# Sharing key rows between tiles, halving the experts' lists, a silu from tanh, and normalized rows remade on chip

## What is computed

```python
xn = layernorm(x)
# attention: q, k, v = heads(xn @ W + b)
scores = (q @ k.T + rel_q + rel_k) / 4     # rel_q[l, r] = q[l] . emb[l - r + 255], rel_k[l, r] = k[r] . emb[...]
s = layer_norm(softmax(scores) @ v @ Wo + bo + xn) * gamma + beta
# experts: n = layer_norm(xn); x1 = xn + n + n @ mix_w + mix_b
y = sum over the two chosen e of w[e] * (silu(z @ w1[e] + b1[e]) @ w2[e] + b2[e])   # z = layer_norm(x1)
g = silu(x1 + y)
out = x + s * g
```

## Time and profile before

| | us |
|---|---|
| median of 3 runs (lowest, highest) | 1816.91 (1814.05, 1818.83) |
| the profiled execution | 1817.45 |
| its span, first to last instruction | 1815.8 |
| TensorE, VectorE, ScalarE, GpSimd busy in it | 1545.8, 1246.4, 1058.4, 583.0 |
| granted TensorE clock, mean share of full speed | 0.934 |

### The profile page before, as it was taken

How to read it: one execution, slowest core, us unless ns; L and a number is a source line. 1 busy time by engine, 2 the same in 40 slices (tenths; PEclk the granted TensorE clock), 3 DMA queues, 4 the chain that set the end, 5 groups by cost and what they waited for, 6 DMA issues and landing times.

```text
span 1815.8 us, 34886 instructions
## 1 busy us (share of the span) xinstructions
PE 1545.8 (85%) x12086; PEld 1164.0 (64%) x12086; DVE 1246.4 (69%) x3120; ACT 1058.4 (58%) x2250; POOL 583.0 (32%) x754
## 2 busy tenths in 40 slices
PE   5759630377999999998999999988999999999996
PEld 2324430366898889897988888955555555555553
DVE  6846643361466666666675667688998899998995
ACT  2425332122655555554555455289898888988983
POOL 1343456241110111110111011124353655636556
PEclk9879755688999999999999999999999999999998
DMA  6454338796899999899999987899989889898891
GB/s 218 162 177 157 134 100 255 192 200 220 251 325 346 313 336 382 283 329 393 391 375 331 374 293 268 301 340 346 302 282 339 304 294 345 281 345 302 294 318 47
DMA packets 218318, 510.49 MB, mean 281 GB/s; under 512 B 28480, under 2 KB 76096, under 8 KB 213664
## 3 DMA queue, kind: packets, MB, share of 16 engines
q1 hardware_dynamic: 193568, 411.58, 66.9%
q0 software_dynamic: 23424, 92.49, 14.6%
q10 hardware_dynamic: 1152, 4.19, 0.6%
HBM read 435.11 MB, written 195.82 MB: 347 GB/s over the span
## 4 chain that ended last, share of the span: by engine, by line
PE 55%; DVE 7%; issue 7%; DMA 5%; ACT 4%; POOL 3%; POOLq 0%; SPq 0%; DVEq 0%; ACTq 0%; another core or an unknown queue 0%
PE up L1120 12%; PE dn L1132 12%; PE rl L1100 11%; PE pt L1517 8%; PE sc L1509 4%; PE cx L1530 4%; DVE rel_out L1048 3%; DMA scratch_rel<-rel_out 2%; DMA rows<-scratch_sorted 2%; DVE probsT L1402 2%; PE wo_ps L1552 1%; ACT square L1359 1%; PE wo_ps L1555 1%; ACT square L1025 1%; PE tp L1108 1%
## 5 line engine op out<-in xcount | busy, mean ns | idle before, releaser
L1048 DVE TENSOR_TENSOR rel_out<-rl,square 128x1024 f32<-128x1024 f32 x256 | 402.5, 1575 | 231.1 <-PE rl L1100 208.8
L1025 ACT COPY square<-rl 128x1024 f32<-128x1024 f32 x256 | 259.5, 1016 | 273.8 <-DVE rel_out L1048 183.8
L1359 ACT ACTIVATE square<-square,row_least 128x512 f32<-128x512 f32 x512 | 365.8, 717 | 21.6 <-DVE row_least L1394 20.0
L1394 DVE CUSTOM_DVE_ANT_1 square<-sc,square 128x512 f32<-128x512 f32 x512 | 338.0, 686 | 36.0 <-issue 32.6
L1517 PE MATMUL pt<-ident,square 128*128 128x128 f32 x2048 | 316.1, 277 | 31.2 <-ACT probsT L1366 24.1
L1120 PE MATMUL up<-rowsT,w_b 128*128 128x128 f32 x2272 | 312.5, 284 | 8.7 <-DVE rowsT L1054 6.8
L1517 PEld LDWEIGHTS pt<-ident,square 128*128 128x128 f32 x2048 | 243.8, 142 | 111.6 <-DVE probsT L1402 36.8
L1132 PE MATMUL dn<-w_b,hid 128*128 128x256 f32 x1136 | 300.6, 393 | 0.0
L1120 PEld LDWEIGHTS up<-rowsT,w_b 128*128 128x128 f32 x2272 | 279.4, 195 | 11.0 <-DVE rowsT L1054 8.3
L1034 ACT ACTIVATE hid<-up,w_b 128x128 f32<-128x128 f32 x568 | 162.6, 372 | 147.9 <-PE up L1120 147.9
L1132 PEld LDWEIGHTS dn<-w_b,hid 128*128 128x128 f32 x1136 | 200.6, 194 | 18.2
(11 more groups left out here) (197 smaller groups left out, 1688.7 us busy)
## 6 DMA issues: line engine op xcount, KB each, us to landing
scratch_rel<-rel_out SPq DMA_DIRECT2D x256, 512.0 KB, 5.2
square<-scratch_rel SPq DMA_DIRECT2D x256, 512.0 KB
w_b<-in_w POOLq DMA_DIRECT2D x71, 1152.0 KB
w_b<-in_w POOLq DMA_DIRECT2D x71, 1028.0 KB
krows_sb<-scratch_stack SPq DMA_DIRECT2D x128, 192.0 KB, 4.9
krows_sb<-scratch_stack SPq DMA_DIRECT2D x128, 128.0 KB, 4.9
late_by_head<-scratch_parts SPq DMA_DIRECT2D x128, 128.0 KB
scratch_parts<-part SPq DMA_DIRECT2D x96, 128.0 KB
```

The source lines that it names most:

```text
L1025: nc.scalar.copy(dst, src).then_inc(s_kc, 1)
L1048: nc.vector.tensor_tensor(out[n % SRING][:], rl[r][:].rearrange("p a (b s) -> p (a b) s", s=TILE), square(tile)[:, u * UN:(u + 1) * UN], A ...
L1359: nc.scalar.activation(sm[j][:, i], sm[j][:, i], ACT.Exp, bias=least[:, j, i:i + 1], scale=-1.0, accum_out=es[:, g // 2 % 2, i, 2 * j + g ...
L1394: nc.vector.tensor_tensor_reduce(sm[j][:, i].rearrange("p (c s) -> p c s", c=LT), sc[i % 2][:].rearrange("p (c s) -> p c s", c=LT), rq[j][ ...
```

## The change

- `project` no longer stores the normalized rows. VectorE keeps each row's mean and inverse deviation (`means`, `invs`). `attention` loads only x, and GpSimd recomputes `xo` from it (`center`), so it waits for that load.
- The gate's silu is written as (1 + tanh(v / 2)) v / 2. ScalarE writes the tanh into `yg`; GpSimd adds 1 and multiplies with `ax` (`twice_silu`, at the end of each batch's round). The factor 1/2 goes once into gamma and beta.
- Block `jb` no longer stands at position jb of the experts' list: even blocks walk through positions 0 to 35, odd ones through 36 to 70 (`part_of`), each with its own weight slot. `fresh` compares neighbouring positions.
- The tiles go forward and backward by turns (`ORDER`), so that the last tile of a row and the first of the next share their key rows; these are loaded once (`RUN`), 13 x 8 pieces instead of 16 x 8. The ring has nine slots, four of them in `late_by_head`. The products begin at block 8.
- SyncE issues the first five key pieces between the loads of the late half, the stack store right after the repacks, and four key pieces and the query rows behind that. The clearing of `late_by_head` moves from block 10 to behind the store of block 68.

```diff
-FIRST_REL = 10
+EVEN = (NBLK + 1) // 2
+FIRST_REL = 8
-KRING = 5
+KRING = 9
+LATE_SLOTS = 4
+ORDER = [(lt, rt if lt % 2 == 0 else LT - 1 - rt) for lt in range(LT) for rt in range(LT)]
...
@@ project
-            def store_xn(b):
-                sp.wait_ge(s_xn, b + 1)
-                sp.dma_start(t["xn"][b * S:(b + 1) * S].rearrange("(p t) e -> p t e", t=ST), xn[:, b * ST:(b + 1) * ST]).then_inc(s_xs[b], 16)
...
+                if half == 1:
+                    step.did(nc.vector.tensor_copy(means[:, p * PAIR:(p + 1) * PAIR], mv[:, :, 0]))
+                    step.did(nc.vector.tensor_copy(invs[:, p * PAIR:(p + 1) * PAIR], y[:, 0:PAIR]))
@@ route
-                then(nc.vector.tensor_tensor(fresh_f[:, 2:NBLK], owner_f[:, 2:NBLK], owner_f[:, 0:NBLK - 2], ALU.not_equal))
+                then(nc.vector.tensor_tensor(fresh_f[:, 1:NBLK], owner_f[:, 1:NBLK], owner_f[:, 0:NBLK - 1], ALU.not_equal))
@@ experts
-        kst = [sb(f"krows_sb{i}", [KS, PIECE, BH], BF16) for i in range(KRING)]
+        kst = [sb(f"krows_sb{i}", [KS, PIECE, BH], BF16) for i in range(KRING - LATE_SLOTS)]
+        for late in by_head:
+            room = late[:].rearrange("k h l -> k (h l)").rearrange("k (n x h) -> k n x h", n=LATE_SLOTS // 2, h=BH)
+            kst += [room[:, i] for i in range(LATE_SLOTS // 2)]
...
+        RUN = [sum(ORDER[i][1] != ORDER[i - 1][1] for i in range(1, tile + 1)) for tile in range(TILES)]
+        LAST_OF = {run: tile for tile, run in enumerate(RUN)}
+        RT_OF = {run: ORDER[tile][1] for tile, run in enumerate(RUN)}
+        LOADS = len(LAST_OF) * PIECES
+        NEW_ROW = [tile == 0 or ORDER[tile][0] != ORDER[tile - 1][0] for tile in range(TILES)]
+        def used(x):
+            return LAST_OF[x // PIECES] * UNITS + (x % PIECES + 1) * PER_PIECE
...
-                    x = ((tile + 1) * UNITS + u) // PER_PIECE - 1 + KRING
-                    if u % PER_PIECE == 0 and x < TILES * PIECES:
+                    while x < LOADS and used(x - KRING) <= (tile + 1) * UNITS + u:
                         load_k(x)
...
+            def part_of(jb):
+                return jb // 2 + jb % 2 * EVEN
...
-                if jb == FIRST_REL:
-                    pool.wait_ge(s_br, B)
-                    for late in keep["late_by_head"]:
-                        nc.gpsimd.memset(late[:].rearrange("k h l -> k (h l)").bitcast(F32), 0.0).then_inc(s_gaps, 1)
...
+                if jb == LAST_REL:
+                    pool.wait_ge(s_kp, TILES * UNITS)
+                    for late in keep["late_by_head"]:
+                        nc.gpsimd.memset(late[:].rearrange("k h l -> k (h l)").bitcast(F32), 0.0).then_inc(s_gaps, 1)
@@ attention
+            step.did(nc.gpsimd.tensor_scalar(gb[:], gb[:], 0.5, None, ALU.mult))
+            def twice_silu(b):
+                own = ax[b % 2][:].rearrange("p t e -> p (t e)")
+                pool.wait_ge(s_g, b + 1)
+                tanh = yg[:].rearrange("p i k e -> p (i k e)")
+                step.did(nc.gpsimd.tensor_scalar(tanh, tanh, 1.0, None, ALU.add))
+                step.settle()
+                step.did(nc.gpsimd.tensor_tensor(own, own, tanh, ALU.mult))
+                step.settle()
...
             def reload(b):
                 after(pool, s_hh, 2 * b)
-                pool.dma_start(xo[:], t["xn"][b * S:(b + 1) * S].rearrange("(p t) e -> p t e", t=ST)).then_inc(s_xo, 16)
                 pool.dma_start(xx[:], t["x"][b * S:(b + 1) * S].rearrange("(p t) e -> p t e", t=ST)).then_inc(s_xx, 16)
+            def center(b):
+                pool.wait_ge(s_xx, (b + 1) * 16)
+                for i in range(ST):
+                    n = b * ST + i
+                    nc.gpsimd.tensor_scalar(xo[:, i], xx[:, i], means[:, n:n + 1], invs[:, n:n + 1],
+                                            ALU.subtract, ALU.mult).then_inc(s_xo, 1)
...
                 if b:
                     reload(b - 1)
+                    center(b - 1)
...
                 if b:
                     finish(b - 1)
+                twice_silu(b)
...
-                nc.scalar.activation(ax[b % 2][:], ax[b % 2][:], ACT.Silu).then_inc(s_g, 1)
+                nc.scalar.activation(yg[:].rearrange("p i k e -> p (i k e)"), ax[b % 2][:].rearrange("p t e -> p (t e)"), ACT.Tanh,
+                                     scale=0.5).then_inc(s_g, 1)
```

More of the change, by code:

```diff
@@ L154, in project @@
         s_ps = [sem(f"parts_stored{i}") for i in range(PRING)]
-        s_xs = [sem(f"xn_stored{i}") for i in range(B)]
         block = ctx.enter_context(nc.Block())
@@ L939, in sync @@
                 sp.dma_start(by_head[b % 2][:], src).then_inc(s_bh[b % 2], 16)
[L940 to L944 removed]
+                if b == 2:
+                    sp.wait_ge(keep["stack_stored"], 16 * 2)
+                if 2 <= b < 2 + KRING - LATE_SLOTS:
+                    load_k(b - 2)
             sp.wait_ge(s_br, B)
@@ L948, in sync @@
                 sp.dma_start(dst, by_row[:, i * TILE:(i + 1) * TILE]).then_inc(s_bs, 16)
+            x = KRING - LATE_SLOTS
+            while x < KRING:
+                load_k(x)
+                x += 1
+            for p in range(PIECES):
+                load_q(0, p)
             sp.wait_ge(s_bs, 16 * 2)
-            for p in range(PIECES - 1):
-                load_k(p + KRING)
+            while used(x - KRING) < UNITS:
+                load_k(x)
+                x += 1
             for tile in range(TILES):
```

56 lines of the change are left out of this document (25 added, 31 removed).

## The result

The changed kernel takes 1824.33 us (median of 6 runs, 1820.74 to 1829.81) where the kernel before takes 1815.73 (6 runs, 1811.84 to 1818.83): a ratio of 1.0049, 95% interval 1.0031 to 1.0066. It is slower by 8.6 us, where 1808 was forecast. The profiled execution took 1829.81 us, span 1828.1, against 1817.45 and 1815.8: +12.3 us to account for. (The profiled execution is the slowest of the six; by the medians it is 8.6.)

The account below looks back on a forecast made before the run. TensorE was taken to hold both long stages, so an edit is worth what it takes from TensorE's waits. Terms 0 - 2 - 17 + 3 - 18 + 10 + 15 = -9 gave 1808 us, range 1789 to 1828.

Parts of the forecast that it names:

- Stored rows gone: Before the experts: eight stores leave SyncE's queue, eight small copies enter VectorE's; 0 us, between -1 and +1.5.
- Blocks 0 to 7: First expert blocks: the earlier stack store may shorten TensorE's 11.27 us wait for rows; -2 us, between -6 and +4.
- Interleaved stretch: Experts with relative products: fewer doubled spots, two disturbed stretches go as weights load less often; -17 us, between -25 and -7.
- Clearing: Start of attention: SyncE's first loads wait until GpSimd has cleared the late rows; +3 us, between +1 and +5.
- GpSimd's additions: GpSimd's round in attention: doubled silu adds 5.6 us (3.9 to 6.1), centring 4.87 us plus the `xx` landing.
- Rival C: GpSimd is quicker: doubled silu 3.9 us, no wait in attention, tail +11; 1794 us, chance 0.20.
- wait at VectorE's addition: Attention, batches 2 to 6: centred rows come 42.9 us after the seed, wanted at 40.86; 2.1 us each, +10 us.
- The gate's -18: Attention's gates: tanh without table loads takes 2.57 of TensorE's 3.1 us wait, seven times; -18 us, between -21 and -15.
- The tail: From the last seed to the final addition: GpSimd's longer chain takes 102.2 us instead of 87.3; +15 us (+11 to +19).
- A: Rival: GpSimd's chain sets attention's period, centred rows 5.3 us late; +11 us, 1828 us, chance 0.15.
- B: Rival: the disturbed expert stretches come from query rows alone and stay, -7 instead of -17; 1818 us, chance 0.17.
- D: Rival: the change does not do what it says, tanh brings its own table loads; given no chance.

Follow-up runs that it names:

- last group: Three kernels timed together, before at 1783.49 us: a base with half lists, one with silu back (1764.04 us), one with normalized rows stored and reloaded (1754.74 us).
- third group: Four kernels timed together, before at 1782.71 us: a base and three undoing half lists (1772.88 us), tile order and shared key rows (1756.33), or both (1770.52).
- best_again: Changed kernel with x loaded ahead of the doubled silu and gathers, the last batch's ahead of the root and centred before that silu: 1760.50 us, 0.9881 of before.
- old_tiles: best_again with tiles row by row, key rows loaded for every tile and late rows cleared early; half lists stay: 1756.33 us, 0.9848 of before.
- base_silu: half_lists_base with silu and its table loads back on ScalarE, no doubled silu on GpSimd, centring kept: 1764.04 us, 0.9889 of before.
- half_lists_base: The old_tiles kernel timed again as a base: 1755.70 us, 0.9842 of before.
- experts_only: Changed kernel's expert stage with attention as before: normalized rows stored and reloaded, silu on ScalarE: 1811.32 us, 0.9946 of before.
- rows_reloaded: Changed kernel with normalized rows stored and loaded again, tangent gate and doubled silu on GpSimd kept: 1797.38 us, 0.9872 of before.
- first group: Four kernels timed together, before at 1820.94 us: changed kernel with gate, stored rows or both put back, or x loaded ahead; 1797.38 to 1811.32 us.
- silu_kept: Changed kernel with silu and its table loads back on ScalarE, rows still centred on chip: 1811.24 us, 0.9946 of before.
- rows_ahead: Changed kernel with x loaded once more, straight into `xo` ahead of the root on GpSimd, and centred in place behind it: 1802.10 us, 0.9895 of before.

## Why the prediction was wrong

**The path, step by step.** *Stored rows gone, 0*: right (1.0 us in the last group, +1.2 before the experts in the trace). *Blocks 0 to 7, -2*: nothing came (+0.1), and in the third group the one kernel whose products begin at block 10 is the fastest there (83.3 us against 87.9 to 96.1), so an earlier start may cost more than it was given. *Interleaved stretch, -17*: right in size (-16.9) and in cause: the two disturbed blocks, 12.5 us longer than plain ones before (11.2 forecast), are gone with the half lists and back without them; the key rows' share of it was nothing. *Clearing, +3*: within its range of 1 to 5, but smaller: from block 70 to the seed of batch 0 `best_again` takes 157.1 us and `old_tiles`, which clears early, 155.5.

*GpSimd's additions*: the doubled silu was 5.57 us (5.6 forecast, with a tensor_scalar of 2.81 instead of 3.2), the centring 4.86 (4.87), the issue of x 30.92 us after the seed (30.87). Rival C, by which GpSimd would be quicker, fell, though its one-input operation did come out somewhat faster than forecast; the rule of the Trainium skill beside it (page "GPSIMD Engine Reference", section "Elementwise — side-by-side cycle accounting") is not borne out: 2.81 us against 2.39 for the two-input tensor_tensor of the same size.

**The step that failed** is the wait at VectorE's addition: +10 forecast. Measured are 28.7 us against the 4.3 that stood there before, so +24.4. It is the difference of two distances from the seed, and both were off. VectorE stood at the addition after 38.53, 38.59, 38.68, 38.66 and 38.33 us in batches 2 to 6. TensorE's result comes 0.86 us later in before and in all runs whose rows are early (in the round shown above TensorE's last product for it ends at 1670.98, 39.2 us after the seed), so the rows were wanted after 39.4 us, not after 40.86. I took that number from the profile before without asking what the change does to it. It held waits that the gate of silu leaves behind the seed: TensorE's 1.87 us wait ends at 1635.41, 0.15 us behind the seed at 1635.26, and VectorE then waits at its next scores (1.01 us in the same place of `base_silu`, shown above). The change removes these. The runs bear it out: from the seed to the addition it goes 40.2 us in `base_silu` and 39.3 in `half_lists_base`, 41.6 in `experts_only` and 39.8 in `rows_reloaded`. So the gain at the gate moved the deadline of the other part of the same change. The other end: rows came, and the addition started, 44.3 us after the seed on average, not 42.9, since x took 7.1 to 9.1 us to land in these batches, mean 8.2, and not 7.2. The price per batch is 4.9 us instead of 2.1, and 2.8 x 5 = 14 us of the 17 that this row of the table misses; the other 3 lie with the gate.

**The gate's -18** was mis-sized too. It took TensorE's waits at the gate, 3.1 us less 0.5, for time of the kernel, by the rule with which the prediction opens (an edit is worth what it takes out of TensorE's waits); in the last group a gate adds 1.8 us to VectorE's waits and as much to the period, 12.5 us for seven. The doubled silu takes some of it back in the tail, which leaves the 8.3 of the last group. In the first group the pair gives 2.4 us a period and 13.9 in all, so the gate's worth is known only as 8 to 14 us.
The changed kernel's own trace hides that. I read its period less the whole wait, 72.7 us, as 2.9 under before, and so expected 20 us from the gates; but 0.86 us of that wait are TensorE's in both, which leaves 2.1. And traces with silu and no wait for rows have periods of 74.4, 75.6, 76.1 and 76.5 us (`base_silu`, before, `silu_kept`, `experts_only`), and VectorE's waits at its score additions in attention, for which the profile names no releaser, rise with them: 29.4, 32.6, 40.3 and 43.3 us. With the tangent it is 72.6 at 18.7 us (`half_lists_base`), 74.1 at 26.3 (`rows_reloaded`) and 75.2 at 34.7 (`rows_ahead`). So a period carries some 2 us that differ between groups and kernels and that I had taken for the gate's; only kernels of one group tell its part. The code waits at those additions for the scores and for the relative rows; which of them the 2 us are, and whether they belong to the chip or the kernel, is not shown.
The Trainium skill's drain of 1.38 us for each switch of tables (page "ScalarE: Activation LUTs", section "What ACT_TABLE_LOAD costs") made the term -37, and the measured -8.3 (and -13.9) is far from that.

**The tail, +15**: right. Seed of batch 5 to the final addition took 101.3 us (102.2 forecast, 87.3 before).

**The rivals.** A is what happened, near the time it gave (1828; the median is 1824.33, the profiled execution 1829.81), by a somewhat different sum: not a doubled silu of 6.1 us and a landing of 9.9, but an earlier deadline and a landing of 8.2. Its point of decision, 44.5 us, rested on the same 40.86; with 39.4 it would have been 43.0, next to my own forecast of 42.9. With nothing but the deadline put right, my figures give 3.5 x 5 = +17.5 in place of +10 and a sum of -1.5: no gain that a measurement could tell. B fell: the disturbed stretches went. D did not occur.

## What to carry to other kernels

When one part of a change lengthens a helper's chain and another shortens the work that chain has to fit beside, work out the deadline anew from the changed program: the slack shrinks from both ends, and the two parts are worth less together than apart. A load whose landing stands on such a chain should be issued as soon as its buffer is free, ahead of the work that stands before its use: here one moved line was worth 40 us. And measure a part's worth with the chain out of the way, not where a wait hides it.

## What the runs showed of the hardware that I had not expected

- The kernel before took 1821 us on one chip and 1783 to 1785 on three others. In two traces of the changed kernel, spans 1828.1 and 1806.3 us, the difference lies ahead of the experts: the first expert block starts at 343.55 and at 320.20, and the periods of attention are 78.4 and 78.3 us.
- A load of 512 KB (x for one batch) took 7.1 to 9.1 us from its issue to the centring in the body of attention of the profile after, and 5.0 us in the tail, where the DMA share is 0.10 (1780 to 1828 us).
- A tensor_scalar on GpSimd of 128x1024 with one immediate took 2.81 us and the tensor_tensor of that size 2.39: of these two, the one with a second input tensor was the faster.
- In `half_lists_base`, where VectorE waits for no rows in batches 1 to 6, the period repeats to within 0.2 us from batch to batch (72.49 to 72.68). That is no rule: in `rows_reloaded`, without such waits either, it goes from 73.71 to 74.57.
